# Local attention layers: GpSimd's order within a tile, sine products ahead of the power

## The reference

```
h = shift_token(x);  q, k, v = split(h @ wqkv)          # 8 heads of 64
q = l2norm(q) * q_scale;  k = l2norm(k) * k_scale       # l2norm: t / |t| for each head
q = q*cos*scale + rotate_half(q)*sin*scale              # k with /scale
o = local_attention(q, k, v)                            # 64 queries see their own and the 64 keys before
x = x + o @ wo
h = layernorm(shift_token(x));  x = x + (a * gelu(g)) @ w2 + b2    # a, g = split(h @ w1 + b1)
```

## Time and profile before

| | us |
|---|---|
| median of 3 runs | 1327.54 |
| lowest and highest | 1327.36, 1328.87 |
| the profiled execution | 1329.68 |
| its span, first to last instruction | 1327.9 |
| busy in the span: TensorE / VectorE | 1224.0 / 1114.4 |
| busy in the span: ScalarE / GpSimd | 920.4 / 757.1 |

### The profile page before, as it was taken

How to read it: one execution, slowest core, us unless ns; L and a number is a source line. 1 busy time by engine, 2 the same in 40 slices (tenths; PEclk the granted TensorE clock), 3 DMA queues, 4 the chain that set the end, 5 groups by cost and what they waited for, 6 DMA issues and landing times. The chain is left out here.

```text
span 1327.9 us, 30439 instructions
## 1 busy us (share of the span) xinstructions
PE 1224.0 (92%) x10593; PEld 714.5 (54%) x10593; DVE 1114.4 (84%) x2919; ACT 920.4 (69%) x2459; POOL 757.1 (57%) x769
## 2 busy tenths in 40 slices
PE   6889999999999999888999999699899999997896
PEld 3634444444444433456666666566466666665663
DVE  6898989998899898689899998665698999997676
ACT  6356777877777787577888888432688888885344
POOL 5212223311322232498999999431799999997244
PEclk9989999999999999999999999899999999998999
DMA  5312331122111101012111111100112111111001
GB/s 133 117 52 63 93 90 54 52 63 64 47 47 39 42 5 59 17 30 51 26 33 33 34 26 34 41 1 1 24 34 55 26 34 33 34 25 25 1 9 56
DMA packets 38848, 56.48 MB, mean 43 GB/s; under 512 B 7187, under 2 KB 23965, under 8 KB 38685
## 3 DMA queue, kind: packets, MB, share of 16 engines
q1 hardware_dynamic: 37880, 54.19, 15.3%
q10 hardware_dynamic: 816, 0.34, 0.2%
HBM read 27.78 MB, written 8.39 MB: 27 GB/s over the span
## 5 line engine op out<-in xcount | busy, mean ns | idle before, releaser
L1176 ACT ACTIVATE a_prob<-a_psE 128x512 f32<-128x512 f32 (+1 forms) x608 | 303.3, 591 | 133.1 <-PE a_psE L775 131.5
L1585 DVE CUSTOM_DVE_ANT_0 a_psM<-a_psM,mask_q 128x384 f32<-128x384 f32 (+3 forms) x512 | 234.6, 522 | 33.3 <-PE a_psM L759 32.8
L1411 POOL TENSOR_SCALAR_AFFINE_SELECT a_prob<-a_prob 128x512 f32<-128x512 f32 x128 | 81.0, 640 | 311.2 <-ACT a_prob L1176 307.4
L1470 POOL TENSOR_TENSOR w_rn<-w_ssm,mhalf 128x16 f32<-128x16 f32 x64 | 220.5, 3446 | 49.9 <-DVE w_ssm L1677 34.6
L775 PE MATMUL a_psE<-a_qs,a_ks 84*128 84x512 bf16 (+3 forms) x768 | 235.9, 330 | 9.4 <-ACT a_prob L1176 6.7
L759 PE MATMUL a_psM<-a_ks,a_qs 72*128 72x512 bf16 (+3 forms) x768 | 235.9, 329 | 4.3 <-DVE a_nm L1585 2.1
L1286 ACT ACTIVATE w_prob<-w_psS,w_bias 128x128 f32<-128x128 f32 x512 | 180.3, 378 | 20.3 <-DVE w_bias L1703 20.3
L1455 POOL TENSOR_TENSOR w_t<-w_raw,w_sin 128x256 f32<-128x256 f32 x252 | 176.4, 731 | 0.0
L1587 DVE TENSOR_REDUCE a_nm<-a_psM 128x1 f32<-128x512 f32 x256 | 158.8, 682 | 12.9 <-PE a_psM L759 11.5
L1460 POOL TENSOR_TENSOR w_rot<-w_t,w_t 128x1024 f32<-128x1024 f32 x63 | 148.6, 2358 | 8.6 <-issue 0.4
L775 PEld LDWEIGHTS a_psE<-a_qs,a_ks 84*128 84x128 bf16 x768 | 73.7, 97 | 144.3 <-ACT a_prob L1176 77.5
(11 more groups left out here) (201 smaller groups left out, 2452.8 us busy)
## 6 DMA issues: line engine op xcount, KB each, us to landing
a_qs<-q_parts SPq DMA_DIRECT2D x32, 288.0 KB
a_ks<-k_parts SPq DMA_DIRECT2D x32, 288.0 KB
q_parts<-p_parts SPq DMA_DIRECT2D x24, 128.0 KB
k_parts<-p_parts SPq DMA_DIRECT2D x24, 128.0 KB
w_vb__699<-w_v__683 SPq DMA_DIRECT2D x16, 128.0 KB, 2.2
w_vb__700<-w_v__683 SPq DMA_DIRECT2D x16, 128.0 KB, 2.3
w_vb__700<-w_v__684 SPq DMA_DIRECT2D x16, 128.0 KB, 2.2
w_vb__701<-w_v__684 SPq DMA_DIRECT2D x16, 128.0 KB, 2.4
```

Source lines behind the costliest of these rows:

```text
L1176: act.activation(prob[G % NPROB][:, j - share + 1:j + 1, 0:w], psE[:, r % NRING, 0:share * w].rearrange("p (j n) -> p j n", j=share), ACT. ...
L1470: pool.tensor_tensor(rn[:, T % 2, 0:n], ssm[:, T % 2, 0:n], sb["mhalf"][:, 0:n], ALU.pow).then_inc(rn_done, 1)
L1585: d = dve.tensor_tensor_reduce(scores, scores, sb["mask_q"][:, 512 - n:512], -1.0, -3.0 * NEG, ALU.add, ALU.min, low)
```

## The change

GpSimd's `rotate` is cut in two: `sines(T)` with the four products and the waits ahead of them, and `add_sines(T)` with the sum and its waits. In the loop over the tiles the order per tile was power, sines, sum; it becomes sines, power, sum. For tile 0 the order stays. The other engines' lists are unchanged.

```diff
-            def rotate(T):
+            def sines(T):
 
                 pool.wait_ge(raw_done, T + 1)
                 ge(pool, rot_done, T)
...
                         i = pool.tensor_tensor(out[:, w, :, half, :], src[:, w, :, 1 - half, :], tab, ALU.mult)
                 i.then_inc(t2_done, 1)
+
+            def add_sines(T):
+
                 pool.wait_ge(t1_done, T + 1)
                 pool.wait_ge(t2_done, T + 1)
                 ge(pool, qkT_done, T - 1)
...
                     norms(0)
-                    rotate(0)
+                    sines(0)
+                    add_sines(0)
...
                 for T in range(layer * NT if layer > 0 else 2, layer * NT + NT):
+                    sines(T)
                     norms(T)
-                    rotate(T)
+                    add_sines(T)
```

## The result

The changed kernel takes 1391.82 us (median of 4 runs, 1391.36 to 1393.14) where the kernel before, beside it on the same chip, takes 1328.2: a ratio of 1.046, interval 1.044 to 1.048. It is slower, by 63.5 us of span in the profiled executions (1391.4 against 1327.9; the profiled run of after took 1393.14 us).

The account below looks back on a forecast made before the run. Before the edit a GpSimd-VectorE ring took 8.86 us a tile, TensorE and ScalarE 8.59. Steady slots cost 60.5 us, layer 1's start gains 0.9: +59.6 on 1329.68 gives 1389, the median 2.1 lower: 1387 us, range 1340 to 1405.

Parts of the forecast that it names:

- The slot: Local layers, from one VectorE normalisation to the next: 10.13 us after the edit, where 8.86 stood.
- 48 steady slots: The steady stretches of both layers, 20 and 28 slots: 425.74 us becomes 486.24, 60.5 more.
- The start of layer 1: A wait of 2.27 us at 953.59 goes, but the first collisions follow: 0.9 us gained.
- early slots of layer 0: Eight long slots before the steady stretch: one wait gained or up to 3 us lost, taken as 0.
- a waiting VectorE gets in between two GpSimd instructions: Shared SBUF access: VectorE enters between gapless GpSimd instructions, so normalisation and division each hold a sine 1.07 us.
- rival (b): GpSimd keeps the SBUF port through consecutive instructions: pairs of slots 17.62 us instead of 17.73, about 1324; chance 0.07.
- (c): Normalisation and division collide with sines part of the time or once a slot: 1340 to 1370; 0.80 together with the forecast.
- Rival (a): The power again covers VectorE's normalisation and division, GpSimd stays within 8.58 us a slot: 1311 us; chance 0.13.
- falls behind in four slots from anywhere: GpSimd loses about 1 us a slot against a reserve of 0.4, so every start ends in 10.13 us slots.
- the lock: Steady order where VectorE's normalisation and division meet GpSimd's sines every slot, each making the other wait: 10.13 us.
- the replay: Slots stepped through from GpSimd ahead, power held by the normalisation, until the slot is 10.13 us.
- The loss of 0.9 us in each second power: Kernel before: one power lasts 3.82 us, the next 2.92, since the normalisation starting 0.16 us earlier holds it.

Follow-up runs that it names:

- e9: The changed kernel with VectorE's normalisation and division replaced by reductions of the same 1024 numbers that read one tensor: 1303.54 us.
- e6: The changed kernel with a second buffer for the sine products, so a tile's first sine no longer waits for the sum ahead of it: 1381.03 us.
- e5: The changed kernel with VectorE's small carry step put ahead of the normalisation: 1352.15 us.
- e10: e5 plus one pause on VectorE in layer 1, seven reductions into unused numbers ahead of tile 37's squared sums: 1331.91 us.
- e8: The changed kernel with VectorE's normalisation and division as instructions of the same output that read one tensor and one number per partition: 1319.79 us.
- e7: The kernel before, with VectorE waiting for its squared norms and filling 128 unused numbers ahead of the normalisation: 1312.19 us, ratio 0.9865.
- e4: The kernel before, with a fill of one number a partition put ahead of VectorE's normalisation: 1330.58 us, ratio 1.000.

## Why the prediction was right

**The slot.** Forecast 10.13 us, measured 10.15, and right step by step. Counted from N's start at 706.68, the first sine ends at 1.82 (forecast 1.77), the fourth at 4.86 (4.80), the power at 7.74 (7.67), the sum at 10.04 (10.03). VectorE's wait of 1.68 us and TensorE's of 1.40 stand where the prediction put them, and no steady power has idle time ahead of it. The 8.59 us that the prediction took as the bound of TensorE and ScalarE is about right: e9's slots are 8.56.

**The sum.** 48 steady slots were to cost 60.5 us and cost 61.3 (25.7 and 35.6). The start of layer 1 was to gain 0.9; tiles 30 to 34 gained 0.5. The early slots of layer 0 were taken at 0 and cost 1.2, within the 3 us that the prediction allowed. The end, taken at 0, gained 0.9. The 2.4 us ahead of tile 2 were in no term; the first N of the changed kernel (549.20) and of the seven experiments with its order lies anywhere from 544.83 to 551.47 us, so a difference of this size there is not put down to the edit. In all +63.5 of span where +59.6 was forecast, and 1391.82 us where 1387 was.

**The step that decided** was that a waiting VectorE gets in between two GpSimd instructions, read from one row. The single sines show it in each steady slot, e6 shows it from the other side (N gets in behind the first sine), and rival (b), for which this had to be false, is out. So is (c): every tile of both stretches has two sines of 1.70 us or more. Rival (a) needed the power to cover N and D again. e5 (layer 0) and e10 show that the new order can run like this, with slots of 8.75 us, once the carry is moved ahead of N so that the power starts first. The changed kernel did not reach it in either layer. That the reason is its N, which starts ahead of the power, rests on e5, where the moved carry alone freed layer 0; a pause in the changed kernel without that move was not run.

**What was too broad.** That GpSimd "falls behind in four slots from anywhere" holds for the changed kernel, where N starts ahead of the power and costs it 0.9 us. It is not a property of the new order: with the power ahead, GpSimd stays ahead (e5 in layer 0), and which order a stretch keeps is decided by how it starts, as long as GpSimd's round is shorter than the slot (in e8 it was 0.03 us longer, and the free order did not last). And in layer 1 the lock came faster than in the replay, after one slot of 6.95 us. That slot is shorter than GpSimd's 8.2 us of work, while the replay started from a slot of 8.6.

**What the forecast passed over.** The loss of 0.9 us in each second power, on which it spent a paragraph as evidence, was also the lever: 0.09 us of head start for the power brings 17 us (e7).

## What to carry to other kernels

Before you move an instruction on GpSimd, write down which VectorE instruction with two SBUF inputs each of its steps runs beside, before and after the move: a step that reads little is the one to keep there, and a dependency count alone would have forecast a gain here. If an engine is fuller for the same instructions, look for two engines that exclude each other, and test it with an instruction of the same length that reads one tensor: a reduction here, since the faster one-source instruction of e8 still held GpSimd. Where two orders both hold themselves, ask in which of them the loop starts, and whether a fraction of a microsecond in the right place chooses the better.

## What the runs showed of the hardware that was not expected

- A power of 16 numbers that starts 0.09 us ahead of N loses nothing (2.91 us, e7), one that starts 0.16 us behind it loses 0.92 (3.83, e4); and N starting 0.09 us behind the power is not held (1.20 us). So it is only at its start that the power and N stand in each other's way.
- A one-source VectorE instruction (`tensor_scalar`) of 0.75 us for 1024 numbers holds GpSimd for 0.45 us; a reduction of 1.21 us over the same numbers doesn't hold it at all (e8, e9).
- Work added on the engine that waits, 8.0 us once, left the stretch from tile 33 to 63 30 us shorter (e10 against e5).
